# Weighted values of an image in one group, two groups a turn in place of four, in a vision transformer's attention loop

## The reference

```python
for i in range(DEPTH):                       # 4 layers, 64 images, 197 tokens, 8 heads of 16
    y = layernorm(h, ln1_w[i], ln1_b[i])
    q, k, v = split(y @ qkv_w[i] + qkv_b[i])
    attn = softmax(einsum('bhnd,bhmd->bhnm', q, k) * scale)
    o = einsum('bhnm,bhmd->bhnd', attn, v)
    h = h + (o @ proj_w[i] + proj_b[i])
    y = gelu(layernorm(h, ln2_w[i], ln2_b[i]) @ fc1_w[i] + fc1_b[i])
    h = h + (y @ fc2_w[i] + fc2_b[i])
return layernorm(h, norm_w, norm_b)
```

## Time and profile before

| | |
|---|---|
| Runs, median (lowest to highest) | 3659.69 us (3652.66 to 3664.78) |
| Profiled execution: its own time / span | 3660.88 / 3659.1 us |
| TensorE matmul, busy | 3379.4 us (92%) |
| TensorE weight load, busy | 2580.2 us (71%) |
| VectorE, ScalarE, GpSimd busy | 2384.5, 2018.8, 2279.2 us (65, 55, 62%) |
| Granted TensorE clock, mean | 0.975 of full |
| Attention turns | 128 |

### The profile page before, as it was taken

The page is one execution under the profiler, slowest core; times in us unless marked ns, Lnnn a source line. Parts: engine busy times, 40 slices in busy tenths (PEclk is TensorE's granted clock), DMA queues, the critical chain, the costliest instruction groups (busy, mean ns, idle before and its releaser), DMA issues. The chain is left out here.

```text
span 3659.1 us, 87958 instructions
## 1 busy us (share of the span) xinstructions
PE 3379.4 (92%) x29756; PEld 2580.2 (71%) x29756; DVE 2384.5 (65%) x6229; ACT 2018.8 (55%) x3948; POOL 2279.2 (62%) x2634
## 2 busy tenths in 40 slices
PE   7999999989999899999999999999899898999983
PEld 4577787777787677777777777777544686766762
DVE  2267777657777666777766677766698677885110
ACT  0156666656666665666665666667465464323331
POOL 0356664576666386666548666637598684377886
PEclk9999999999999999999999999999999899999997
DMA  6856675046766315766703666640111133143443
GB/s 221 271 110 127 127 132 104 9 84 127 132 129 127 60 28 105 129 127 127 131 12 61 123 128 127 130 82 1 39 33 27 54 83 58 35 105 74 68 62 32
DMA packets 456073, 342.26 MB, mean 94 GB/s; under 512 B 70659, under 2 KB 440171, under 8 KB 455595
## 3 DMA queue, kind: packets, MB, share of 16 engines
q1 hardware_dynamic: 404419, 275.69, 38.9%
q10 hardware_dynamic: 24224, 46.44, 3.9%
q0 software_dynamic: 27136, 16.42, 3.4%
HBM read 227.68 MB, written 109.29 MB: 92 GB/s over the span
## 5 line engine op out<-in xcount | busy, mean ns | idle before, releaser
L795 DVE TENSOR_REDUCE a_neg_max<-a_S 99x4 f32<-99x788 f32 x1024 | 1003.7, 980 | 484.9 <-PE a_S L346 481.3
L558 ACT ACTIVATE a_shared<-a_St 99x792 f32<-99x792 f32 (+1 forms) x1024 | 851.2, 831 | 637.2 <-PE a_St L363 626.0
L363 PE MATMUL a_St<-a_q_st,a_k_st 99*99 99x198 bf16 (+1 forms) x4096 | 527.8, 251 | 55.4 <-DMA a_q_st<-a_max_rows 39.1
L346 PE MATMUL a_S<-a_k_st,a_q_st 96*99 96x197 bf16 x4096 | 538.7, 254 | 39.4 <-DVE a_neg_max L795 39.4
L346 PEld LDWEIGHTS a_S<-a_k_st,a_q_st 96*99 96x99 bf16 x4096 | 390.0, 126 | 255.0 <-DVE a_neg_max L795 216.8
L382 PE MATMUL a_O<-a_shared,a_v_aug 99*32 99x198 f32 (+1 forms) x8192 | 464.8, 339 | 0.4
L363 PEld LDWEIGHTS a_St<-a_q_st,a_k_st 99*99 99x99 bf16 (+1 forms) x4096 | 390.3, 126 | 84.9 <-DMA a_q_st<-a_max_rows 48.1
L707 POOL CAST a_parts<-a_q_k 128x792 bf16<-128x792 f32 x128 | 107.8, 842 | 321.3 <-issue 281.2
L382 PEld LDWEIGHTS a_O<-a_shared,a_v_aug 99*32 99x32 f32 (+1 forms) x8192 | 247.0, 110 | 84.3 <-issue 1.8
L687 POOL CAST a_max_parts<-a_neg_max 99x32 bf16<-99x32 f32 x128 | 26.8, 210 | 406.7 <-DVE a_neg_max L795 406.7
L498 PEld LDWEIGHTS a_O<-a_w,a_shared 128*99 128x99 f32 x2048 | 243.2, 167 | 40.8 <-issue 23.1
(11 more groups left out here) (271 smaller groups left out, 7312.4 us busy)
## 6 DMA issues: line engine op xcount, KB each, us to landing
a_shared<-in_x ACTq DMA_DIRECT2D x64, 594.0 KB, 5.0
spill_q<-a_parts SPq DMA_DIRECT2D x384, 99.0 KB
spill_k<-a_parts SPq DMA_DIRECT2D x384, 99.0 KB
a_k_st<-spill_k SPq DMA_DIRECT2D x128, 297.0 KB, 4.0
a_q_st<-spill_q SPq DMA_DIRECT2D x128, 297.0 KB, 6.2
a_k_st<-spill_k SPq DMA_DIRECT2D x128, 198.0 KB, 4.6
a_q_st<-spill_q SPq DMA_DIRECT2D x128, 198.0 KB, 6.7
a_k_st<-spill_k SPq DMA_DIRECT2D x128, 99.0 KB, 4.9
```

What stands on the lines that cost most here:

```text
L346: mm = nc.tensor.matmul(S[0:TC, j // 2, j % 2 * TB:j % 2 * TB + NTOK], q_st[p % 4][0:SPLIT, head, b * TB + c * TC:b * TB + (c + 1) * TC], ...
L363: mm = nc.tensor.matmul(St[0:keys, j // 2, j % 2 * TB:(j % 2 + 1) * TB], k_st[p][:, head, first:first + keys], q_st[p][:, head, b * TB:(b ...
L558: nc.scalar.activation(probs[0:keys, u % 4, :].rearrange("p (x t) -> p x t", x=2), St[0:keys, :, 0:2 * TB], ACT.Exp).then_inc(s["probs"], 1)
L795: nc.vector.tensor_reduce(out.rearrange("p (x y) -> p x y", x=2), S[0:TC, :, 0:2 * TB].rearrange("p x (y t) -> p x y t", y=2)[:, :, :, 0:N ...
```

## The change

The two groups of an image are issued one behind the other: those of image 1 of the previous pair after slot 0, those of image 0 after slot 4. `probs` gets a fifth place, and two tables say which place an exponential writes and how many groups it waits for. `turned`, then `o_turn` of the previous pair's image 1, stand ahead of slot 3 (the latter stood behind it); q and `max_turned` stand ahead of slot 4; v is made in two halves, before and after slot 6; `o_turn` of image 0 moves from after slot 7 to before it. k is made in M2 in place of M0 from turn 0 on. ScalarE's copies are ordered anew between the exponentials: o_copy of image 1 ahead of exponential 1, oT_copy ahead of 2, the copy to yT ahead of 3, o_copy of image 0 ahead of 5, and oT_copy ahead of 6. On VectorE only the border between two pieces moves. SP and GpSimd are untouched.

```diff
--- before.py
+++ after.py
@@ -137,6 +137,8 @@
 TURNED_PART, MAXED_PART = 1, 2
 NORM_AT = (1, 6, 11, 16, 21, 26)
 NORMED = len(NORM_AT)
+PROBS_AT = (3, 0, 1, 4, 2, 0, 1, 4)
+PROBS_FREE = (-3, -1, 0, 0, -1, 1, 2, 2)
 
 
 def layers_phase(nc, g, A):
@@ -185,9 +187,9 @@
         conv_w, cT = conv_w.rearrange("p (k d) -> p k d", d=D), [cT0, cT1]
 
         probs, gl0, gl1, m_xn0, m_xn1, m_yT0, m_yT1, oT0, oT1, o_sb, o_n = places(
-            [(TC, 16 * TB), (128, 2 * PW), (128, 2 * PW), (TC, 4 * D), (TC, 4 * D), (128, PW), (128, PW),
+            [(TC, 20 * TB), (128, 2 * PW), (128, 2 * PW), (TC, 4 * D), (TC, 4 * D), (128, PW), (128, PW),
              (128, PW), (128, PW), (128, PW), (TC, 2 * D)])
-        probs, o_n = probs.rearrange("p (u t) -> p u t", u=4), o_n.rearrange("p (c d) -> p c d", d=D)
+        probs, o_n = probs.rearrange("p (u t) -> p u t", u=5), o_n.rearrange("p (c d) -> p c d", d=D)
         gl = [x.rearrange("p (h t) -> p h t", h=2) for x in (gl0, gl1)]
         m_xn = [x.rearrange("p (t d) -> p t d", d=D) for x in (m_xn0, m_xn1)]
         m_yT, oT = [m_yT0, m_yT1], [oT0, oT1]
@@ -381,7 +383,7 @@
                             keys = TC - c
                             mm = nc.tensor.matmul(O[32 * j:32 * j + 32, half * TB:(half + 1) * TB],
                                                   v_aug[p % 4][0:keys, 2 * b + c, half * 4 + j, :],
-                                                  probs[0:keys, 2 * half + c, j * TB:(j + 1) * TB],
+                                                  probs[0:keys, PROBS_AT[4 * b + 2 * half + c], j * TB:(j + 1) * TB],
                                                   start=(c == 0), stop=(c == 1))
                     mm.then_inc(s["pv"], 1)
 
@@ -425,70 +427,78 @@
 
                     slot(0)
                     if last:
+                        pv(l, i - 1, p - 1, 1, 0)
                         pv(l, i - 1, p - 1, 1, 1)
                     slot(1)
                     if last:
                         oT_turn(l, i - 1, 0)
                     if live(-2):
                         wait(pe, s["oT"], 2 * at(l, i - 1))
-                        wait(pe, s["k_f"], at(l, i + 5))
-                        peeled(i, ("v_aug", at(l, i + 3)), ("q_f", at(l, i + 4)))
+                        wait(pe, s["v_aug"], at(l, i + 3))
                         for t in range(4):
                             mm = nc.tensor.matmul(M0[0:TC, t * D:(t + 1) * D], oT[p % 2][:, t * TC:(t + 1) * TC], m.wp,
                                                   start=True, stop=True)
                         mm.then_inc(s["proj"], 1)
                     slot(2)
-                    if now:
-                        pv(l, i, p, 0, 0)
                     yield
                     if live(5):
                         wait(pe, s["xn"], at(l, i + 6))
-                        wait(pe, s["max_copied"], at(l, i + 1))
-                        peeled(i, ("yT", at(l, i + 5)), ("m_yT", y(TURNED_PART)))
+                        wait(pe, s["k_f"], at(l, i + 5))
+                        peeled(i, ("yT", at(l, i + 5)), ("max_copied", at(l, i + 1)), ("m_yT", y(TURNED_PART)))
                         for t in range(4):
                             mm = nc.tensor.transpose(M2[:, t * TC:(t + 1) * TC], xn[:, t, :], g.ident[0:TC, 0:TC])
                         mm.then_inc(s["turned"], 1)
-                    slot(3)
                     if last:
                         o_turn(l, i - 1, 1)
+                    slot(3)
                     if live(4):
                         wait(pe, s["h_done"], at(l, i - 1))
                         peeled(i, ("k_f", at(l, i + 5)), ("v_aug", at(l, i + 3)))
                         nc.tensor.matmul(M0[:, 0:PW], m.wq, yT[p][:], start=True, stop=True).then_inc(s["q"], 1)
-                    slot(4)
                     yield
                     if nxt:
                         wait(pe, s["max_split"], 4 * at(l, i + 2))
                         wait(pe, s["yT"], at(l, i + 6))
-                        peeled(i, ("max_copied", at(l, i + 1)), ("m_yT", y(MAXED_PART)))
+                        peeled(i, ("k_f", at(l, i + 5)), ("max_copied", at(l, i + 1)), ("m_yT", y(MAXED_PART)))
                         nc.tensor.matmul(M2[0:96, 0:TC], max_parts[:].rearrange("p k n -> p (k n)"), ident[:],
                                          start=True, stop=True).then_inc(s["max_turned"], 1)
+                    slot(4)
                     if now:
+                        pv(l, i, p, 0, 0)
                         pv(l, i, p, 0, 1)
                     slot(5)
                     if last:
                         oT_turn(l, i - 1, 1)
+
+                    def v(t0):
+                        for t in (t0, t0 + 1):
+                            mm = nc.tensor.matmul(M0[0:TC, t * D:(t + 1) * D], yT[(p + 3) % 4][:, t * TC:(t + 1) * TC], m.wv,
+                                                  start=True, stop=True)
+                        return mm
+
                     if live(3):
                         wait(pe, s["q_f"], at(l, i + 5))
                         peeled(i, ("h_done", at(l, i - 1)), ("k_f", at(l, i + 5)))
-                        for t in range(4):
-                            mm = nc.tensor.matmul(M0[0:TC, t * D:(t + 1) * D], yT[(p + 3) % 4][:, t * TC:(t + 1) * TC], m.wv,
-                                                  start=True, stop=True)
-                        mm.then_inc(s["v"], 1)
-                    yield
+                        v(0)
                     slot(6)
-                    if now:
-                        pv(l, i, p, 1, 0)
-                    slot(7)
+                    if live(3):
+                        v(2).then_inc(s["v"], 1)
                     if now:
                         o_turn(l, i, 0)
+                    yield
+                    slot(7)
                     if live(5):
                         wait(pe, s["yT"], at(l, i + 6))
-                        wait(pe, s["v_aug"], at(l, i + 4))
-                        peeled(i, ("q_f", at(l, i + 5)), ("k_f", at(l, i + 5)), ("h_done", at(l, i - 1)))
                         if isinstance(i, int) and i < 0:
+                            wait(pe, s["v_aug"], at(l, i + 4))
+                            wait(pe, s["q_f"], at(l, i + 5))
+                            wait(pe, s["k_f"], at(l, i + 5))
                             wait(pe, s["w_done"], l + 1)
-                        nc.tensor.matmul(M0[:, 0:PW], m.wk, yT[(p + 1) % 4][:], start=True, stop=True).then_inc(s["k"], 1)
+                            to = M0
+                        else:
+                            wait(pe, s["max_copied"], at(l, i + 2))
+                            to = M2
+                        nc.tensor.matmul(to[:, 0:PW], m.wk, yT[(p + 1) % 4][:], start=True, stop=True).then_inc(s["k"], 1)
 
                 def mlp(l, k, turned, maxed):
                     m = layer_w[l]
@@ -554,8 +564,8 @@
                 def exp(l, i, u):
                     keys = TC - u % 2
                     wait(act, s["scores_t"], 8 * at(l, i) + u + 1)
-                    wait(act, s["pv"], 4 * at(l, i) + u // 2 - 1)
-                    nc.scalar.activation(probs[0:keys, u % 4, :].rearrange("p (x t) -> p x t", x=2),
+                    wait(act, s["pv"], 4 * at(l, i) + PROBS_FREE[u])
+                    nc.scalar.activation(probs[0:keys, PROBS_AT[u], :].rearrange("p (x t) -> p x t", x=2),
                                          St[0:keys, :, 0:2 * TB], ACT.Exp).then_inc(s["probs"], 1)
 
                 def o_copy(l, i, b):
@@ -579,34 +589,36 @@
                     if live(4):
                         wait(act, s["k"], at(l, i + 5))
                         wait(act, s["lo"], at(l, i + 4))
-                        nc.scalar.activation(q_k[:, 1, :], M0[:, 0:PW], ACT.Identity, bias=m.bk).then_inc(s["k_f"], 1)
+                        made = M0 if isinstance(i, int) and i <= 0 else M2
+                        nc.scalar.activation(q_k[:, 1, :], made[:, 0:PW], ACT.Identity, bias=m.bk).then_inc(s["k_f"], 1)
+                    if last:
+                        o_copy(l, i - 1, 1)
                     if now:
                         exp(l, i, 1)
                     if last:
-                        o_copy(l, i - 1, 1)
+                        oT_copy(l, i - 1, p - 1, 0)
                     if now:
                         exp(l, i, 2)
                     yield
-                    if last:
-                        oT_copy(l, i - 1, p - 1, 0)
-                    if now:
-                        exp(l, i, 3)
                     if live(5):
                         wait(act, s["turned"], at(l, i + 6))
                         wait(act, s["v"], at(l, i + 2))
                         nc.scalar.activation(yT[(p + 1) % 4][:], M2[:, 0:PW], ACT.Copy).then_inc(s["yT"], 1)
                     if now:
+                        exp(l, i, 3)
+                    yield
+                    if now:
                         exp(l, i, 4)
-                    yield
```

(5 more changed lines are left out.)

## The result

The changed kernel takes 3717.62 us (median, 3709.78 to 3723.28) beside 3656.18 of the kernel before in the same comparison: ratio 1.0166, 95% interval 1.0147 to 1.0186, so 61 us slower. Forecast was 3697 with 3668 to 3728.

The account below looks back on a forecast made before the run. TensorE and the single score buffer's wait were taken to bound the attention turns together. Longer turns and edges gave +85 us, less 48 of DMA stops, so +37: 3697 us, range 3668 to 3728.

Parts of the forecast that it names:

- The bound: Attention turns: TensorE bounds the undisturbed 14.02 us turn, and the wait on the single score buffer is met at once.
- the score ring: One score buffer: scores of the next slot wait for VectorE's row maximum, so no slot is shorter than 1.58 to 1.62 us.
- The saving of a pair: Two weighted-values groups issued together on TensorE: 0.22 us saved per pair, the pair costing 1.57 us.
- The fourth rival: Weighted-values pairs: the second group drains the first after all, adding 50 us, 3747; chance 0.05.
- The slots: Eight stretches of a turn, scores to next scores: 14.67 us in sum in the loop, 2.38 each for slots 0 and 4.
- The first rival: Attention turns: TensorE's sum decides, 13.60 us of work a turn, so faster at 3630 to 3640; chance 0.10.
- light slots: Slots 2, 5 and 7 of a turn: under 1.55 us they would prove the forecast wrong.
- The fifth rival: A moved wait bites, above all in slots 0 and 4: 0.1 to 0.3 us a turn, 3705 to 3730; chance 0.08.
- The stops: Transposed scores waiting for the row maxima's DMA: about 56 us before the change, 48 of it given back.
- The second rival: No change: the score buffer's wait costs its lowest, 1.58 us, and all DMA stops vanish, 3665 or so; chance 0.07.
- the third: Rival: DMA stops stay, as landings follow slot 4 rather than the reads; 3744, or 3720 with half the relief; chance 0.10.
- Edges: Turns at the layers' ends: +14 us in turns 27 to 29, +8 in 30 and 31, -3 in the first turn.

## Why the prediction was right, and where it was short

**The bound** (right). TensorE's order and the score ring met at once: the kernel before kept its turn with a shorter maximum, the changed kernel did not.

**The saving of a pair** (right). 0.22 a pair forecast. By recorded busy time it is 464.8 - 414.1 = 50.7 us over 256 pairs, 0.20; by the distances between starts, with a pair at 1.52 in place of 1.57, it is 0.27. The fourth rival is out. The Trainium skill (TensorEngine Tiling (Array Packing), Key Properties) says that a change of tiling mode drains the array. The trace agrees that the way in and out of a group costs something, 0.20 for each one taken away; it does not show that this is a drain, and the time does not follow it.

**The slots** (right). The sum was 14.67 against 14.58 measured, nearly all of it in the two pairs' 0.05 each; the six other slots came out within 0.01. The growth was thus 0.55 a turn and not 0.65, which is some 8 us less over turns 1 to 26. The first rival wanted light slots under 1.55: they are at 1.58 and above, and fall under it only with the ring cut. Its 13.60 of work doesn't match the prices listed, which add up to 13.81 over the eight slots, as several slots carry the slower scores after a gap. The fifth rival wanted slots 0 and 4 longer than priced; they last 2.34 and 2.33.

**The stops** (right in size, half right in reason). 48 us of relief forecast; the entry went from 48.1 to 8.4 us of brackets, which at 1.17 is 47, of which some 12 are within what this entry does between executions. The second rival (the ring at 1.58 throughout, no stop left) and the third (the stops stay) are out. Of the two reasons given, only one is shown. The reads decide: an earlier issue gained nothing, and with no read in flight the landing is 2.1 us. That a longer turn helps because the reads then end earlier against slot 0 fits the landing, 3.3 us in place of 3.8 in the median, but no run changes the turn's length alone.

**Edges** (their sum right by luck). Turns 30 and 31 were forecast at +8 and gave +16. At full clock they are 1.2 and 0.7 longer, as forecast (1.3 and 0.8). The other 8 us are clock: one turn 30 has 15.5 us at a granted clock of 0.75 and three turns 31 have 12.9 to 14.2 at 0.87, 0.76 and 0.79, where 13.4 and 11.3 are those at 1.00; of the kernel before only one turn 31 is under 1.00 (0.90). Turns 27 to 29 were forecast at +14 and, with their own stops relieved, gave +5. Turn 0 was forecast at -3 and gave -7, and not for the reason given: nearly all of it is gained in the two layers in which its clock does not fall at all (13.7 us at 1.00 in place of 16.7 at 0.71), and the kernel before with the new borders shows the same with no group moved. These errors cancel, and nothing in the forecast made them.

**The step that was short.** The attention turns gave +36 against +37 for the whole kernel, in part because the errors above cancel. The sum had no term for the turns below 0. I had read the change's moved `yield`s only as an order, and the order is indeed the same; but in those turns a yield decides what stands between two feed-forward steps, and there nothing covers the ring. The changed kernel lost 23 us there by the trace (with the part behind the layers 6 us shorter); with the old borders 25 us of the span came back. The border also changes where the clock falls: some of the 7 us gained in turn 0 belong to it. This and not the ring's size is most of why the median lies at 3718 and not at 3697; some 4 us are the difference between medians and profiled executions. The border on VectorE stood in the description of the change and had no price in the sum.

**What to look for** (two wrong). I had expected TensorE to be busy less by 50 us. The weighted values were; the engine as a whole shows 30 us more, so its busy time was no measure of the saving. The stops under 10 us, the pair and the slots came as said. An idle bracket on the light slots' first scores was expected on five rows and is absent from most of them.

## What to carry to other kernels

Where an engine's own work and a ring through a second engine are equally long in every slot, work can't be taken out at one place and put in at another for nothing: price each slot as the longer of the engine's own work and the ring, and sum those. An order written in pieces has to be priced once for each way in which the pieces are run. Here a small transfer that landed late behind large ones was mended by moving the large ones out of its way, and only when both left early enough; neither an earlier issue nor another queue did it alone.

## What the runs showed of the hardware

Weighted values on a quarter of the columns each: a group of 16 starts costs 0.83 us alone and a pair of 32 starts 1.52. A 6.2 KB transfer landed 2.1 us (median) after its issue with no stack read in flight; behind 1.2 MB of reads on the same queue it took 3.8 us in the kernel before, and 5.4 when it was issued 1.7 us earlier; from ScalarE's queue beside those reads 3.3 to 4.0 in the median and up to 7.1. Between feed-forward steps TensorE's granted clock fell to 1.2 GHz (0.59 and 0.56 in the two stretches above) after score groups with waits of 1.28 and 0.64 us, and the drop cost about 0.8 us on the next 16 matmuls (2.75 against 1.91). In the kernel before with the new borders waits of 1.28 and 0.20 us at the same place were not followed by a fall.
